# A third expert stage with four buffers, two banks for spread and sum, and second products five blocks behind

## The chip, the cores and the metric

The kernel runs on one core of a Trainium2 chip. The core has a matrix engine (PE), a vector engine (DVE), a scalar engine (ACT), a general engine (POOL) and a queue that issues transfers (SP). Each engine takes its instructions in the order in which they were written; between engines only semaphores hold work back. Products are written to eight banks of PSUM, each of 128 x 512 float32 numbers here. The metric is the time of one execution on the device, in microseconds (us).

## The reference

Four layers of a small model work on 2048 tokens of width 128; each layer is a mixing step and then a feed-forward step, both on a normalised input and both added back. The change touches the feed-forward step of the third layer only, a mixture of 8 experts with 256 hidden units, of which each token uses two:

```python
logits = xf @ Wg + bg
probs = jax.nn.softmax(logits, axis=-1)
w, idx = jax.lax.top_k(probs, TOP_K)
w = w / jnp.sum(w, axis=-1, keepdims=True)
comb = jnp.sum(jax.nn.one_hot(idx, E, dtype=xf.dtype) * w[..., None], axis=1)
h = jax.nn.relu(jnp.einsum('nd,edh->enh', xf, W1) + b1[:, None, :])
y = jnp.einsum('enh,ehd->end', h, W2) + b2[:, None, :]
out = jnp.einsum('end,ne->nd', y, comb)
```

The kernel computes all experts for all tokens and weighs the hidden units by `comb`, which is zero for experts that a token does not use.

## The kernel before

The tokens are cut into four chunks of 512 (`NC` = 4, `CH` = 512). The stage of the third layer is called FFN2; its 8 x 256 hidden units are 16 blocks of 128, two for each expert. For each chunk `c` and block `b` (number `n` over all of them) the work is this, with features along the partitions and tokens along the 512 columns:

- **first product** (`up`, PE): the block's 128 x 128 weights by the normalised input, into the gate bank `n % 2`. Every product is three matmuls (`mm3`, lines 731 to 733), since weights and inputs are each held as a high and a low part: high by high, high by low, low by high.
- **activation** (`act`, ACT, line 913): bias and Relu from the gate bank into `AO[n % 2]`.
- **spread** (`spread`, PE, line 866): for every second block one matmul that copies an expert's routing weights to all 128 partitions, into the one bank `SP`. It waits until the weighing before it has read the bank.
- **weighing** (`weigh`, DVE, line 968): the activation times the spread bank, into `HO[n % 3]`. It waits until the low part of block n-3 has been made.
- **high part** (`high`, ACT, line 921): a rounded copy of the weighed block into `rbuf[n % 2]`. It waits until the second product of block n-2 has been read from there.
- **low part** (`low`, POOL, line 989; the last two of the stage on DVE): weighed block minus high part, into `rbuf[2 + n % 2]`.
- **second product** (`down`, PE, lines 731 to 733 again): three matmuls that add the block's share to the sum in the one bank `Y`. The first block of a chunk is led by two matmuls with the second bias (lines 877 and 878), and waits until ACT has copied the chunk before out of `Y` (`result`, line 926).

The order within an engine is written out. On PE iteration `b` issues `up(b)`, for even b `spread(b)`, and then `down(b - 3)`, because `_f.lag` is 3. On ACT it issues `act(b)` and `high(b - 1)`, on DVE `weigh(b)`, on POOL `low(b - 2)`. After that come the steps of other work that `hooks` puts at this block, by the table `STEPS_AT`: for the chunk after this one the routing weights, for the chunk two further the normalisation. Steps 0, 1, 11, 2 and 3 are that normalisation (statistics on DVE, a small power on POOL at lines 497 and 498, the scaling on DVE at line 406, four transposes on PE at line 698, the split into high and low on ACT and DVE). Step 4 is twelve narrow matmuls for the logits (lines 719 to 721), 5 to 9 the choice of the two experts (ACT and DVE, lines 444 to 481; the last of them, at b = 11, makes `SC2` in four small copies and four small subtractions, lines 478 and 481), and 10 the four transposes of `SC2` on PE (line 726) with ACT's copy of them into `SCT` (line 545), from which the next chunk's spreads read. The step -1 is the tail of the chunk before: four transposes of its sum on PE (line 749) at b = 3, and the addition on DVE (line 762) at b = 4. POOL also splits the weights of later stages into high and low after every third block, as long as there are any (`work`, lines 2117 and 2118). During the last chunk `hook(EARLY + b)` adds the first five products of the next stage ("keys"), with ACT's copies at line 1606 and DVE's splits at lines 1619 and 1621.

The first chunk starts while the stage before ends; the stage after starts when ACT has copied the last chunk's sum (line 926). For the other two expert stages, which have two first products for each block, the same functions are used with `f.gate` set.

Of the kernel before, what the change touches and what calls it, by code (L numbers as in the profile page):

```python
# [132 lines left out]
for _f in FFNS:  # L133
    _f.block0, _f.spread0, _f.router0 = _blk, _sp, _rt
    _blk += NC * _f.blocks
    _sp += NC * _f.spread
    _rt += NC * (1 if _f.experts else 0)
    _f.lag = 3
ROUTED = {f.norm: f for f in FFNS if f.experts}


def build(nc, x_in, w_split, w_exact, w_raw, out):
    with ExitStack() as ctx:
# [635 lines left out]
        AO = [buf[0], buf[1]]  # L779
        MO = [buf[2], buf[3]]  # L780
        HO = [buf[4], buf[5], buf[6]]

        def body_start(eng, t, c):

# [13 lines left out]
        def in_stage(f, c, b, depth):  # L798
# [5 lines left out]

# [3 lines left out]
        }  # L808
        EARLY = 20
        ALL_STEPS = (0, 1, 11, 2, 3, 4, 5, 6, 7, 8, 9, 10)  # L810
# [19 lines left out]
        def ffn_pe(pe, f, c, hook):  # L830
# [24 lines left out]
            def spread(c, b):  # L855
                if b == f.plain_block or b % f.spread_every:
                    return
                n = block_no(f, c, b)
                if b == 0:
                    pe.wait_ge(weights_sb, f.router0 + c + 1)  # L860
                if in_stage(f, c, b, 1):
                    pe.wait_ge(h_ready, n)
                elif f is FFN2:
                    body_start(pe, f.tail, 0)
                o = EXACT_AT["sel16"][0] + b // f.spread_every * P
                nc.tensor.matmul(SP[:, :], WE[:, o:o + P], SCT[:, bass.ds(c % 2 * CH, CH)],  # L866
                                 start=True, stop=True).then_inc(spread_full, 1)

            def down(c, b):
                n = block_no(f, c, b)  # L870
                if b == 0:
                    y_bank_free(pe, f.tail, c)
                    if f.experts == 8:

                        s = SCT[:, bass.ds(c % 2 * CH, CH)]
                        bh, bl = wh("b2_2")
                        nc.tensor.matmul(Y[:, :], bh, s, start=True, stop=False)
                        nc.tensor.matmul(Y[:, :], bl, s, start=False, stop=False)
# [18 lines left out]
        def ffn_act(a, chain, f, c, hook):  # L897
# [6 lines left out]
            def act(c, b):  # L904
                n = block_no(f, c, b)
                a.wait_ge(first_full, n + 1)
                if in_stage(f, c, b, 2):

                    a.wait_ge(mul_done if f.gate else h_ready, n - 1)
                if f.gate:  # L910
                    nc.scalar.activation(AO[n % 2], G[n % 2][:, :], ACT.Silu).then_inc(act_done, 1)  # L911
                else:
                    nc.scalar.activation(AO[n % 2], G[n % 2][:, :], ACT.Relu, bias=raw("b1_2", b, 1))\  # L913
                        .then_inc(act_done, 1)

            def high(c, b):
                n = block_no(f, c, b)
                a.wait_ge(h_ready, n + 1)
                if in_stage(f, c, b, 2):
                    a.wait_ge(down_done, n - 1)  # L920
                nc.scalar.activation(rbuf[n % 2][:, :], HO[n % 3], ACT.Copy).then_inc(hh_ready, 1)  # L921

            def result(c):
                yt_free(a, f.tail, c)
                a.wait_ge(down_done, block_no(f, c, f.blocks - 1) + 1)
                nc.scalar.activation(YT[:, :], Y[:, :], ACT.Identity, bias=zero).then_inc(yt_ready, 1)
# [17 lines left out]
        def ffn_dve(v, chain, f, c, hook):  # L944
# [12 lines left out]
            def weigh(c, b):  # L957

                n = block_no(f, c, b)
                v.wait_ge(mul_done if f.gate else act_done, n + 1)  # L960
                if in_stage(f, c, b, 3):
                    v.wait_ge(hl_ready, n - 2)
                src = MO[n % 2] if f.gate else AO[n % 2]
                if b == f.plain_block:
                    nc.vector.tensor_copy(HO[n % 3], src).then_inc(h_ready, 1)
                else:
                    v.wait_ge(spread_full, f.spread0 + f.spread * c + b // f.spread_every + 1)
                    nc.vector.tensor_tensor(HO[n % 3], src, SP[:, :], ALU.mult).then_inc(h_ready, 1)  # L968

            for b in range(f.blocks):  # L970
                if f is FFN0 and (c, b) == (0, 1):
# [12 lines left out]
        def low(e_, eng, f, n):  # L984

            eng.wait_ge(hh_ready, n + 1)
            if e_ is nc.vector and n:
                eng.wait_ge(hl_ready, n)
            e_.tensor_tensor(rbuf[2 + n % 2][:, :], HO[n % 3],  # L989
                             rbuf[n % 2][:, :].bitcast(F32), ALU.subtract).then_inc(hl_ready, 1)  # L990

        def low_on_pool(f, c, b):

# [1311 lines left out]
```

## Time and profile before

| what | value |
|---|---|
| three executions, median | 897.65 us |
| lowest and highest of them | 897.23 and 898.66 us |
| the profiled execution | 897.48 us |
| its span, first to last instruction | 895.7 us |
| busy PE, DVE, ACT, POOL over the span | 734.7, 675.6, 575.3, 394.1 us |
| mean granted TensorE clock | 0.911 |

The profiled execution took 897.48 us, of which the span of instructions is 895.7 us; the rest lies before and after them. The stage of the change fills some 145 us of it, from the first weighing at 452.7 us to the copy of the last sum at 598.0 us. A matmul of 512 columns is listed with 0.39 to 0.40 us although the next one starts 0.23 us after it, since matmuls are pipelined: what PE costs is read from start to start.

### The profile page before, as it was taken

What the parts mean: (1) busy time and instruction counts of PE and PEld (TensorE: products, weight loads), DVE (VectorE), ACT (ScalarE), POOL (GpSimd) and SP (SyncE); (2) the same over time, 40 slices, a digit from 0 to 9 for tenths busy, and PEclk for the clock granted to TensorE, in tenths of its full rate; (3) what the DMA queues carried; (4) which work ended last, traced back from release to release, by engine and by line L of the source; (5) the groups of instructions that cost most, each with busy time, mean ns of one, the idle gap of its engine ahead of it and who ended that gap; (6) DMA issues with size and microseconds to landing.
All of it is one profiled execution on the core that took longest, in us unless ns stands there. A gap on an engine that the chain in (4) does not pass through costs nothing. (4 is left out here: it accounts for less than half of the span.)

```text
span 895.7 us, 11019 instructions
## 1 busy us (share of the span) xinstructions
PE 734.7 (82%) x3306; PEld 467.0 (52%) x3306; DVE 675.6 (75%) x1615; ACT 575.3 (64%) x926; POOL 394.1 (44%) x427
## 2 busy tenths in 40 slices
PE   4778998779999889999678888867777767777787
PEld 3666765345545567777555666642232222222575
DVE  6685776798898748787756667769898788786785
ACT  4264664657474535565636667767899979777776
POOL 6638654634445015544248767634333332230330
PEclk9999998988696869999969999998999889789999
DMA  4200001000000000000000000000000000000001
GB/s 134 69 12 15 15 15 33 19 23 24 12 25 19 1 0 1 1 1 0 1 13 23 1 1 0 1 0 1 1 0 1 1 1 0 1 0 1 1 1 48
DMA packets 9610, 11.59 MB, mean 13 GB/s; under 512 B 720, under 2 KB 5712, under 8 KB 9552
## 3 DMA queue, kind: packets, MB, share of 16 engines
q1 hardware_dynamic: 9552, 10.89, 4.2%
q8 instruction: 27, 0.44, 0.2%
q14 instruction: 31, 0.25, 0.1%
HBM read 9.84 MB, written 1.05 MB: 12 GB/s over the span
## 5 line engine op out<-in xcount | busy, mean ns | idle before, releaser
L989 POOL TENSOR_TENSOR rbuf<-B,rbuf 128x512 fp32r<-128x512 f32 x126 | 164.2, 1307 | 101.8 <-ACT rbuf L921 101.0
L968 DVE TENSOR_TENSOR B<-B,spread_bank 128x512 f32<-128x512 f32 x128 | 87.1, 682 | 47.2 <-ACT B L913 33.0
L921 ACT ACTIVATE rbuf<-B 128x512 fp32r<-128x512 f32 x132 | 83.0, 628 | 49.0 <-PE y_bank L733 38.8
L497 POOL TENSOR_SCALAR small<-small 128x4 f32<-128x4 f32 x32 | 8.1, 252 | 175.9 <-DVE small L387 175.7
L731 PE MATMUL y_bank<-rbuf,WH 128*128 128x512 f32 x150 | 64.2, 428 | 20.8 <-POOL rbuf L989 14.4
L955 DVE TENSOR_TENSOR B<-B,up_banks 128x512 f32<-128x512 f32 x68 | 46.5, 684 | 45.4 <-PE up_banks L733 28.5
L911 ACT ACTIVATE B<-gate_banks 128x512 f32<-128x512 f32 x68 | 40.8, 599 | 61.6 <-PE gate_banks L733 60.4
L1715 ACT ACTIVATE B<-B,VEC 128x1024 f32<-128x1024 f32 x48 | 55.2, 1150 | 22.3 <-DVE B L1710 22.3
L731 PE MATMUL gate_banks<-XH,WH 128*128 128x512 f32 x152 | 66.7, 439 | 0.8 <-ACT YT L1313 0.8
L733 PE MATMUL gate_banks<-XH,WL 128*128 128x512 f32 x152 | 62.4, 411 | 0.0
L732 PE MATMUL gate_banks<-XL,WH 128*128 128x512 f32 x152 | 61.9, 407 | 0.0
L1203 POOL TENSOR_SCALAR B<-S,WR 128x128 f32<-128x128 f32 x64 | 39.2, 629 | 49.7 <-DVE S L1185 38.1
L733 PE MATMUL y_bank<-rbuf,WL 128*128 128x512 f32 x150 | 60.2, 402 | 0.0
L732 PE MATMUL y_bank<-rbuf,WH 128*128 128x512 f32 x150 | 60.0, 400 | 0.0
L1617 POOL TENSOR_SCALAR WH<-WK 128x512 fp32r<-128x512 f32 x22 | 13.8, 628 | 104.6 <-issue 57.9
L1244 PEld LDWEIGHTS spread_bank<-VB,B 128*128 128x128 f32 x256 | 37.6, 226 | 34.1 <-issue 26.2
L866 PE MATMUL spread_bank<-SCT,WE 128*128 128x512 f32 x96 | 42.6, 444 | 10.7 <-DVE B L968 8.7
L1716 ACT ACTIVATE B<-B 128x1024 f32<-128x1024 f32 x48 | 50.5, 1052 | 0.0
L913 ACT ACTIVATE B<-gate_banks,WR 128x512 f32<-128x512 f32 x64 | 43.8, 687 | 10.0 <-PE gate_banks L733 9.5
L731 PEld LDWEIGHTS y_bank<-rbuf,WH 128*128 128x128 f32 x150 | 28.9, 193 | 40.2 <-POOL rbuf L989 23.2
L1221 PE MATMUL gate_banks<-B,S 128*64 128x512 f32 x128 | 44.6, 786 | 5.3 <-issue 3.8
L1244 PE MATMUL spread_bank<-VB,B 128*128 128x36 f32 x256 | 41.1, 314 | 2.0 <-DVE Z L1380 2.0
(318 smaller groups left out, 2110.8 us busy)
## 6 DMA issues: line engine op xcount, KB each, us to landing
STG<-in_w_split SPq DMA_DIRECT2D x27, 256.0 KB, 2.7
X<-in_x SPq DMA_DIRECT2D x4, 256.0 KB, 4.6
out<-X SPq DMA_DIRECT2D x4, 256.0 KB, 2.3
WR<-in_w_raw SPq DMA_DIRECT2D x1, 524.5 KB, 4.0
STG<-in_w_exact SPq DMA_DIRECT2D x2, 256.0 KB, 2.7
STG<-in_w_split SPq DMA_DIRECT2D x5, 64.0 KB, 1.9
STG<-in_w_split SPq DMA_DIRECT2D x1, 192.0 KB, 2.3
STG<-in_w_split SPq DMA_DIRECT2D x1, 128.0 KB, 2.1
```

The lines of the kernel that those rows point to most:

```text
L731: nc.tensor.matmul(dst, w[0], x[0], start=start, stop=False)
L732: nc.tensor.matmul(dst, w[0], x[1], start=False, stop=False)
L733: return nc.tensor.matmul(dst, w[1], x[0], start=False, stop=stop)
L913: nc.scalar.activation(AO[n % 2], G[n % 2][:, :], ACT.Relu, bias=raw("b1_2", b, 1))\
L921: nc.scalar.activation(rbuf[n % 2][:, :], HO[n % 3], ACT.Copy).then_inc(hh_ready, 1)
L955: nc.vector.tensor_tensor(MO[n % 2], AO[n % 2], U[n % 2][:, :], ALU.mult).then_inc(mul_done, 1)
L968: nc.vector.tensor_tensor(HO[n % 3], src, SP[:, :], ALU.mult).then_inc(h_ready, 1)
L989: e_.tensor_tensor(rbuf[2 + n % 2][:, :], HO[n % 3], rbuf[n % 2][:, :].bitcast(F32), ALU.subtract).then_inc(hl_ready, 1)
L1221: i = nc.tensor.matmul(G[u][w * WIN:(w + 1) * WIN, :], QN[c_ % 2][:, tok], KM[tile % 2][:, HU * u:HU * u + HU, w * WIN:(w + 1) * WIN], sta ...
L1244: i = nc.tensor.matmul(SP[:, pr * 36:(pr + 1) * 36], PT[u][:, q * P:(q + 1) * P], VB[:, tile % TL, pr, :, :, :].rearrange("p a b d -> p (a ...
L1715: nc.scalar.activation(CS[p % 4], AB[p % 4], ACT.Sin, scale=-TURN, bias=half_pi).then_inc(cos_ready, 1)
L1716: nc.scalar.activation(SN[p % 4], RB[p % 4], ACT.Sin, scale=-TURN).then_inc(sin_ready, 1)
```

## The change

The second products of FFN2 stand five blocks behind the first ones, not three (`_f.lag`). Activations, weighed blocks, high and low parts of this stage have four buffers each: `AO4` and `HO4` take eight of the slots of `B`; two of the four high and low parts are `rbuf` as before, and two lie in columns of `WH` and `WL` whose weights (the taps and those of the second layer) are no longer read. The spread has the bank `SP` and the second half of `up_banks`, in turn; the sum has `Y` for even chunks and the first half of `up_banks` for odd ones, so that only chunks 2 and 3 wait for a copy, that of the chunk two before. The high part is made two blocks behind the activation instead of one. The waits follow: `act(n)` waits for the weighing n-4 (before: n-2), `weigh(n)` for the low part n-4 (n-3), `high(n)` for the second product n-4 (n-2), a spread for the weighing three blocks back (one). Step 10 is at b = 14 instead of 13. By the lag, the copy of a chunk's sum moves from b = 2 of the next chunk to b = 4 on ACT, its transposes from b = 3 to b = 5 on PE, and its addition from b = 4 to b = 6 on DVE. Number and size of the instructions stay as they are.

```diff
-    _f.lag = 3
+    _f.lag = 5 if _f is FFN2 else 3
...
+        MADE_H, MADE_L = (w_[:, _end - 2 * CH:_end] for w_ in (WH, WL))
+        AO4, HO4 = [buf[k] for k in range(4)], [buf[4 + k] for k in range(4)]
+        HI4 = [rbuf[0][:, :], rbuf[1][:, :], MADE_H[:, 0:CH], MADE_H[:, CH:2 * CH]]
+        LO4 = [rbuf[2][:, :], rbuf[3][:, :], MADE_L[:, 0:CH], MADE_L[:, CH:2 * CH]]
+        SP2, Y2 = [SP[:, :], U[1]], [Y[:, :], U[0]]
...
+            return AO4[n % 4] if deep_of(f) else AO[n % 2]
...
+            return HO4[n % 4] if deep_of(f) else HO[n % 3]
...
+            return (HI4[n % 4], LO4[n % 4]) if deep_of(f) else (rbuf[n % 2][:, :], rbuf[2 + n % 2][:, :])
...
+            return SP2[b // f.spread_every % 2] if deep_of(f) else SP[:, :]
...
+            return Y2[c % 2] if deep_of(f) else Y[:, :]
...
-            16: {0: (0,), 1: (4,), 2: (1,), 3: (5,), 4: (11,), 5: (6,), 7: (2, 7), 8: (3,), 9: (8,), 11: (9,), 13: (10,)},
+            16: {0: (0,), 1: (4,), 2: (1,), 3: (5,), 4: (11,), 5: (6,), 7: (2, 7), 8: (3,), 9: (8,), 11: (9,), 14: (10,)},
...
-                if in_stage(f, c, b, 1):
+                if deep_of(f) and in_stage(f, c, b, 4):
+                    pe.wait_ge(h_ready, n - 2)
+                elif deep_of(f):
+                    body_start(pe, f.tail, 0)
+                elif in_stage(f, c, b, 1):
                     pe.wait_ge(h_ready, n)
-                elif f is FFN2:
-                    body_start(pe, f.tail, 0)
...
                 if b == 0:
-                    y_bank_free(pe, f.tail, c)
+                    if not deep_of(f):
+                        y_bank_free(pe, f.tail, c)
+                    elif c > 1:
+                        pe.wait_ge(yt_ready, count(f.tail, c - 1))
...
-                mm3(Y[:, :], wh(f.down, b * P), (rbuf[n % 2][:, :], rbuf[2 + n % 2][:, :]),
+                mm3(dst, wh(f.down, b * P), parts(f, n),
                     b == 0 and f.experts != 8, b == f.blocks - 1).then_inc(down_done, 1)
...
+                    if in_stage(f, c, b, 4):
+                        a.wait_ge(h_ready, n - 3)
+                    nc.scalar.activation(act_out(f, n), G[n % 2][:, :], ACT.Relu, bias=raw("b1_2", b, 1))\
                         .then_inc(act_done, 1)
...
                 a.wait_ge(h_ready, n + 1)
-                if in_stage(f, c, b, 2):
+                if deep_of(f):
+                    if in_stage(f, c, b, 4):
+                        a.wait_ge(down_done, n - 3)
+                elif in_stage(f, c, b, 2):
                     a.wait_ge(down_done, n - 1)
...
-                for at_ in lagged(f, c, b, 2 if f.gate else 1):
+                for at_ in lagged(f, c, b, 2):
                     high(*at_)
...
-                if in_stage(f, c, b, 3):
+                if deep_of(f):
+                    if in_stage(f, c, b, 4):
+                        v.wait_ge(hl_ready, n - 3)
+                elif in_stage(f, c, b, 3):
                     v.wait_ge(hl_ready, n - 2)
```

The order on PE around the first second product of chunk 1. In the kernel before, after `up(3)`; `y_bank` is the sum's bank, and each row names in brackets what it waits for:

```order
L731 MATMUL gate_banks<-XH,WH 128x512 [waits act_done]
L732 MATMUL gate_banks<-XL,WH 128x512
L733 MATMUL gate_banks<-XH,WL 128x512
L877 MATMUL y_bank<-SCT,WH 128x512 [waits yt_ready]
L878 MATMUL y_bank<-SCT,WL 128x512
L731 MATMUL y_bank<-rbuf0,WH 128x512 [waits hl_ready]
L732 MATMUL y_bank<-rbuf2,WH 128x512
L733 MATMUL y_bank<-rbuf0,WL 128x512
L749 MATMUL norm_bank<-WR,YT 128x128 [waits res_done,x32_ready,yt_ready]
L749 MATMUL norm_bank<-WR,YT 128x128 x3
```

In the changed kernel, after `up(5)`:

```order
L731 MATMUL gate_banks<-XH,WH 128x512 [waits act_done]
L732 MATMUL gate_banks<-XL,WH 128x512
L733 MATMUL gate_banks<-XH,WL 128x512
L912 MATMUL up_banks<-SCT,WH 128x512
L913 MATMUL up_banks<-SCT,WL 128x512
L731 MATMUL up_banks<-rbuf0,WH 128x512 [waits hl_ready]
L732 MATMUL up_banks<-rbuf2,WH 128x512
L733 MATMUL up_banks<-rbuf0,WL 128x512
L749 MATMUL norm_bank<-WR,YT 128x128 [waits res_done,x32_ready,yt_ready]
L749 MATMUL norm_bank<-WR,YT 128x128 x3
```

The two bias matmuls and the product now go to the other bank, without a wait for the copy of chunk 0 (`yt_ready`), and the transposes of that copy still follow directly behind the product, two blocks later than before.

PE around the transposes of the routing weights, the step that moved by one block. Before, `down(10)`, the step, and `up(14)` with its spread:

```order
L731 MATMUL y_bank<-rbuf0,WH 128x512 [waits hl_ready]
L732 MATMUL y_bank<-rbuf2,WH 128x512
L733 MATMUL y_bank<-rbuf0,WL 128x512
L726 MATMUL route_bank<-WR,SC2 128x128 [waits weights_tok]
L726 MATMUL route_bank<-WR,SC2 128x128 x3
L731 MATMUL gate_banks<-XH,WH 128x512 [waits act_done]
L732 MATMUL gate_banks<-XL,WH 128x512
L733 MATMUL gate_banks<-XH,WL 128x512
L866 MATMUL spread_bank<-SCT,WE 128x512 [waits h_ready]
```

In the changed kernel, `up(14)` with its spread, `down(9)`, and the step:

```order
L731 MATMUL gate_banks<-XH,WH 128x512 [waits act_done]
L732 MATMUL gate_banks<-XL,WH 128x512
L733 MATMUL gate_banks<-XH,WL 128x512
L897 MATMUL up_banks<-SCT,WE 128x512 [waits h_ready]
L731 MATMUL y_bank<-rbuf1,WH 128x512 [waits hl_ready]
L732 MATMUL y_bank<-rbuf3,WH 128x512
L733 MATMUL y_bank<-rbuf1,WL 128x512
L726 MATMUL route_bank<-WR,SC2 128x128 [waits weights_tok]
L726 MATMUL route_bank<-WR,SC2 128x128 x3
```

`up(14)` and its spread stood behind the step and stand ahead of it now; what lies between the step and the next chunk is `up(15)` and `down(10)` (`up(14)`, `down(11)`, `up(15)` and `down(12)` before).

## Rows read from the trace of the kernel before

**Rows 1.** Busy time by stretch, from each chunk's first weighing to the next one's:

```profile
core 0: us, PE busy (x) PEld busy (x) DVE busy (x) ACT busy (x) POOL busy (x), PEclk, DMA share, GB/s
452.68:490.33 37.65, 32.07 (x123) 23.30 (x121) 23.67 (x61) 21.01 (x34) 28.18 (x27) 0.86 0.08 22
490.33:525.20 34.87, 30.05 (x132) 21.99 (x133) 23.36 (x59) 22.41 (x36) 26.28 (x23) 1.00 0.00 1
525.20:559.20 34.00, 29.51 (x132) 21.80 (x131) 23.39 (x72) 22.53 (x36) 23.39 (x21) 1.00 0.00 0
559.20:593.80 34.60, 30.57 (x129) 22.21 (x127) 24.04 (x51) 24.65 (x39) 22.40 (x20) 1.00 0.00 1
```

**Rows 2.** Waits from 484 to 596 us: total, times, longest, in us:

```profile
ACT rbuf L921 <- PE y_bank L733: 27.4, 30, 2.2
DVE B L968 <- ACT B L913: 25.4, 24, 2.1
POOL rbuf L989 <- ACT rbuf L921: 23.7, 27, 1.6
...
PE route_bank L726 <- DVE SC L481: 2.2, 3, 0.8
...
PE y_bank L877 <- ACT YT L926: 1.3, 2, 0.7
```

**Rows 3.** PE in order of time: start, duration, line, operands:

```profile
484.50 0.66 PE L726 MATMUL route_bank<-WR,SC 128*128 128x128 f32 x4 [0.58 <-DVE SC L481]
484.91 0.47 PE L731 MATMUL gate_banks<-XH,WH 128*128 128x512 f32 x1
...
492.54 0.17 PE L719 MATMUL route_bank<-WH,XH 128*128 128x8 f32 x1
...
493.79 0.48 PE L731 MATMUL gate_banks<-XH,WH 128*128 128x512 f32 x1
...
497.25 0.50 PE L877 MATMUL y_bank<-SCT,WH 128*128 128x512 f32 x1 [0.67 <-ACT YT L926]
...
497.82 0.40 PE L731 MATMUL y_bank<-rbuf,WH 128*128 128x512 f32 x1
...
578.28 0.39 PE L866 MATMUL spread_bank<-SCT,WE 128*128 128x512 f32 x1
578.51 0.40 PE L731 MATMUL y_bank<-rbuf,WH 128*128 128x512 f32 x1
...
579.22 0.39 PE L731 MATMUL route_bank<-XH,WH 128*128 128x512 f32 x1
```

**Rows 4.** ACT in order of time, at the end of the stage:

```profile
592.38 0.63 ACT L921 ACTIVATE rbuf<-B 128x512 fp32r<-128x512 f32 x1 [0.66 <-PE y_bank L733]
593.01 0.69 ACT L913 ACTIVATE B<-gate_banks,WR 128x512 f32<-128x512 f32 x1
593.77 0.63 ACT L921 ACTIVATE rbuf<-B 128x512 fp32r<-128x512 f32 x1
...
597.96 0.69 ACT L926 ACTIVATE YT<-y_bank,VEC 128x512 f32<-128x512 f32 x1 [1.84 <-PE y_bank L733]
```

**Rows 5.** POOL in order of time, at the start and within the first chunk:

```profile
456.50 0.19 POOL L497 TENSOR_SCALAR small<-small 128x4 f32<-128x4 f32 x1 [13.99 <-DVE small L387]
...
457.76 1.27 POOL L989 TENSOR_TENSOR rbuf<-B,rbuf 128x512 fp32r<-128x512 f32 x1
...
479.66 0.62 POOL L2117 TENSOR_SCALAR WH<-STG 128x512 fp32r<-128x512 f32 x1
...
481.64 2.51 POOL L989 TENSOR_TENSOR rbuf<-B,rbuf 128x512 fp32r<-128x512 f32 x2
```

**Rows 6.** DVE in order of time: start, duration, line, operands:

```profile
449.02 0.41 DVE L478 CAST SC<-small 128x16 fp32r<-128x16 f32 x4
...
480.35 2.59 DVE L478 CAST SC<-small 128x16 fp32r<-128x16 f32 x4
482.97 1.47 DVE L481 TENSOR_TENSOR SC<-small,SC 128x16 f32<-128x16 f32 x4
...
496.10 3.56 DVE L406 TENSOR_SCALAR XN<-X,small 128x128 f32<-128x128 f32 x4
```

More of the change, by code:

```diff
@@ L781, in build, with deep_of, act_out, hidden @@
         HO = [buf[4], buf[5], buf[6]]
+        MADE_H, MADE_L = (w_[:, _end - 2 * CH:_end] for w_ in (WH, WL))
[3 more added lines that the diff above has]
+        SP2, Y2 = [SP[:, :], U[1]], [Y[:, :], U[0]]
+        def deep_of(f):
+            return f is FFN2
+        def act_out(f, n):
+            return AO4[n % 4] if deep_of(f) else AO[n % 2]
+        def hidden(f, n):
+            return HO4[n % 4] if deep_of(f) else HO[n % 3]
+        def parts(f, n):
+            return (HI4[n % 4], LO4[n % 4]) if deep_of(f) else (rbuf[n % 2][:, :], rbuf[2 + n % 2][:, :])
+        def spread_bank(f, c, b):
+            return SP2[b // f.spread_every % 2] if deep_of(f) else SP[:, :]
+        def sum_bank(f, c):
+            return Y2[c % 2] if deep_of(f) else Y[:, :]
         def body_start(eng, t, c):
@@ L870, in down @@
                 n = block_no(f, c, b)
+                dst = sum_bank(f, c)
                 if b == 0:
-                    y_bank_free(pe, f.tail, c)
+                    if not deep_of(f):
+                        y_bank_free(pe, f.tail, c)
+                    elif c > 1:
+                        pe.wait_ge(yt_ready, count(f.tail, c - 1))
                     if f.experts == 8:
@@ L876, in down @@
                         bh, bl = wh("b2_2")
-                        nc.tensor.matmul(Y[:, :], bh, s, start=True, stop=False)
-                        nc.tensor.matmul(Y[:, :], bl, s, start=False, stop=False)
+                        nc.tensor.matmul(dst, bh, s, start=True, stop=False)
+                        nc.tensor.matmul(dst, bl, s, start=False, stop=False)
                 pe.wait_ge(hl_ready, n + 1)
-                mm3(Y[:, :], wh(f.down, b * P), (rbuf[n % 2][:, :], rbuf[2 + n % 2][:, :]),
+                mm3(dst, wh(f.down, b * P), parts(f, n),
                     b == 0 and f.experts != 8, b == f.blocks - 1).then_inc(down_done, 1)
@@ L906, in act @@
                 a.wait_ge(first_full, n + 1)
-                if in_stage(f, c, b, 2):
-                    a.wait_ge(mul_done if f.gate else h_ready, n - 1)
                 if f.gate:
-                    nc.scalar.activation(AO[n % 2], G[n % 2][:, :], ACT.Silu).then_inc(act_done, 1)
-                else:
-                    nc.scalar.activation(AO[n % 2], G[n % 2][:, :], ACT.Relu, bias=raw("b1_2", b, 1))\
+                    if in_stage(f, c, b, 2):
+                        a.wait_ge(mul_done, n - 1)
+                    nc.scalar.activation(act_out(f, n), G[n % 2][:, :], ACT.Silu).then_inc(act_done, 1)
+                else:
+                    if in_stage(f, c, b, 4):
+                        a.wait_ge(h_ready, n - 3)
+                    nc.scalar.activation(act_out(f, n), G[n % 2][:, :], ACT.Relu, bias=raw("b1_2", b, 1))\
                         .then_inc(act_done, 1)
@@ L918, in high @@
                 a.wait_ge(h_ready, n + 1)
-                if in_stage(f, c, b, 2):
+                if deep_of(f):
+                    if in_stage(f, c, b, 4):
+                        a.wait_ge(down_done, n - 3)
+                elif in_stage(f, c, b, 2):
                     a.wait_ge(down_done, n - 1)
-                nc.scalar.activation(rbuf[n % 2][:, :], HO[n % 3], ACT.Copy).then_inc(hh_ready, 1)
+                nc.scalar.activation(parts(f, n)[0], hidden(f, n), ACT.Copy).then_inc(hh_ready, 1)
             def result(c):
@@ L925, in result @@
                 a.wait_ge(down_done, block_no(f, c, f.blocks - 1) + 1)
-                nc.scalar.activation(YT[:, :], Y[:, :], ACT.Identity, bias=zero).then_inc(yt_ready, 1)
+                nc.scalar.activation(YT[:, :], sum_bank(f, c), ACT.Identity, bias=zero).then_inc(yt_ready, 1)
             for b in range(f.blocks):
@@ L988, in low @@
                 eng.wait_ge(hl_ready, n)
-            e_.tensor_tensor(rbuf[2 + n % 2][:, :], HO[n % 3],
-                             rbuf[n % 2][:, :].bitcast(F32), ALU.subtract).then_inc(hl_ready, 1)
+            hi, lo = parts(f, n)
+            e_.tensor_tensor(lo, hidden(f, n), hi.bitcast(F32), ALU.subtract).then_inc(hl_ready, 1)
         def low_on_pool(f, c, b):
```

8 lines of the change are left out of this document (4 added, 4 removed).

## The prediction

> **What bounds the kernel now.** I read first the busy time by stretch, cut at each chunk's first weighing [rows 1]. A chunk of the stage takes 37.7, 34.9, 34.0 and 34.6 us, the last one counted only to its last weighing, and in none of them is an engine full: in the second, PE is busy for 30.1 us, POOL for 26.3, DVE for 23.4 and ACT for 22.4. The granted clock is 1.00 from the second chunk on, 2.4 GHz, so the idle time does not cost clock there. PE's 30.1 us count the ends of pipelined matmuls; what it needs comes from starts.
>
> Then the waits [rows 2]: ACT's high part waits 30 times, 27.4 us, for a second product on PE; DVE's weighing 24 times, 25.4 us, for the activation on ACT; POOL's low part 27 times, 23.7 us, for the high part on ACT. Each engine waits for the next one round a ring. That is what a loop with too few buffers looks like: second product n-2, high part n, low part n, second product n. The ring is short of places, not of engine time.
>
> **What each engine needs for a chunk.** PE, from start to start [rows 3]: a product of three matmuls is 579.22 - 578.51 = 0.71 us; I use 0.70, as the time between two starts there is 0.23 to 0.24. A spread is 578.51 - 578.28 = 0.23, the two bias matmuls 497.82 - 497.25 = 0.57, the twelve logit matmuls 493.79 - 492.54 = 1.25, four transposes 484.91 - 484.50 = 0.41. A middle chunk has 32 products, 8 spreads, the bias, the logits and three groups of transposes: 22.4 + 1.8 + 0.6 + 1.25 + 1.2 = 27.3 us. The last chunk has no logits and no routing weights to transpose, but five products and four transposes for the next stage: 22.4 + 1.8 + 0.6 + 1.2 + 3.5 = 29.5 us.
>
> ACT has a high part and an activation in 593.77 - 592.38 = 1.39 us [rows 4], 0.07 more than their 0.63 and 0.69 us; 16 times that on top of its busy 22.4 us makes 23.5 us. POOL has a low part in half of 2.51 us, 1.26 us, so 20.1 us for 16. A split piece of a later weight takes 481.64 - 479.66 = 1.98 us and the small pair of the normalisation 457.76 - 456.50 = 1.26 us [rows 5]. The first chunk has five such pieces, one of them half as large (9.4 us, as I estimate it), the second two. DVE's busy time is the 23.4 to 24.0 us of rows 1. So with enough buffers PE is the bound in the second to fourth chunk, and POOL in the first.
>
> **The change, part by part.** No instruction is added or dropped; it only moves waits.
>
> Four buffers and lag 5. The activation, weighing, high part and low part of a block take 0.69 + 0.69 + 0.63 + 1.26 = 3.3 us [rows 4, 5] (the weighing is 0.69 too, as ACT's activation; it is the same size). In the new order the high part of block n stands on ACT behind the activation of block n+2, two blocks of PE or some 3.0 us later; so from the end of `up(n)` to the end of its low part I count 3.0 + 0.7 + 0.1 + 0.63 + 1.26 = 5.7 us, with 0.1 for the semaphore. `down(n)` comes five blocks of 1.51 us behind, 7.6 us. Nearly 2 us of slack are left in a full PE, and about 4 us for a late weighing, since the high part waits for its turn anyway. With lag 3 PE arrived after 4.5 us, and every hold of DVE reached it at once. Four buffers for the activation let ACT and PE run on by two blocks more while DVE is held. I take these waits as gone except where DVE is held longer than that.
>
> The second sum bank. The waits of PE for ACT's copy are 1.3 us in this stretch [rows 2], once for each chunk change; they go. The second spread bank takes the spread's wait for the weighing just before it. Both are parts of PE's idle 34.9 - 27.3 = 7.6 us and are not counted again.
>
> What stays late: DVE. Its operations from SBUF to SBUF stretch while POOL works. The four small copies of step 9 took 0.41 us with POOL idle at 449 us, but 2.59 us at 480 us, and the four subtractions behind them 1.47 us; the four scalings at 496 us took 3.56 us [rows 6]. POOL gets denser, so I count them as held in every chunk. Step 9 then holds DVE for 4.1 us and 0.7 us of small operations ahead of them, 4.8 us, behind `weigh(11)`. At the end of `weigh(11)` PE is in block 12, with about 4 us of work until `down(9)`, which is just ahead of the transposes. DVE comes to the step late by another 0.4 us or so, from splitting the input at b = 8. So PE waits 1.2 us there, although the step is one block later; it was 2.2 us in three [rows 2], so this wait grows by 0.5. Behind it, `up(15)` and `down(10)` cover the copy into `SCT` less well than the four products of before; weighing 12, high part 12 and the copy, which I take at a high part's length, take 0.69 + 0.63 + 0.63 = 1.95 us against 0.4 + 3 x 0.7 = 2.5 us of PE, so it stays hidden.
>
> The tail. The transposes at b = 5 fill the norm bank, DVE empties it at b = 6, and step 2 needs it on PE at b = 7. Before there were three blocks between them. From the end of `up(6)` PE needs 0.23 + 3 x 0.7 = 2.3 us to step 2, DVE's chain activation, weighing, addition 0.2 + 0.69 + 0.69 + 0.69 = 2.3 us, and DVE is still late from the scalings at b = 2. I take 1.0 us of waiting; it is between 0 and the 3.6 us of the scalings.
>
> Together PE needs 27.3 + 1.2 + 1.0 = 29.5 us for a middle chunk. The second falls from 34.9 to 29.5, a gain of 5.4 us, the third from 34.0, 4.5 us.
>
> The first chunk. The half clock at its start (0.86 as mean of the stretch, 1.2 GHz in part) and the late first low part at 457.76 are as before. From there POOL needs 20.1 + 9.4 = 29.5 us and perhaps 1 us of holds, so the next chunk's first low part can start at 488.3; its weighing stands some 3 us earlier, at 485.3 instead of 490.3. Gain 5.0 us.
>
> The last chunk. From first to last weighing PE has 15 of 16 blocks, 29.5 - 1.5 = 28.0 us, and 1.0 us for the tail step: 29.0 instead of 34.6, 5.6 us. Behind the last activation, though, come six second products and three high parts, two of them one block later than before; POOL's low part 13 ends later and DVE's two wait for it. From the last activation to the copy there were 597.96 - 593.01 = 4.95 us [rows 4]; I add 0.6 us.
>
> Sum: 5.0 + 5.4 + 4.5 + 5.6 - 0.6 = 19.9 us. The stages behind start that much earlier and are not touched. The profiled execution took 897.48 us, 0.17 below the median of 897.65, which changes nothing: 897.5 - 19.9 = **877.6 us**; I say 878.
>
> **A rule that speaks against it.** The held DVE operations are on the trace as said [rows 6]. The Trainium skill ("SBUF — State Buffer", section "Who interferes with whom") says why: VectorE and GpSimd share one pair of SBUF ports under a lock that is held for a whole instruction, and the loser stands still; it concerns copies and scalings in the fast modes and operations with two inputs in SBUF. The trace agrees in that four copies went from 0.41 to 2.59 us. Read strictly it would make every such operation wait out one POOL instruction once POOL has no gaps, and that is the rival "slower" below. The weighing has one input in PSUM and stays out of it by the same rule.
>
> **The rivals.**
>
> *DVE becomes the bound.* It is busy for 23.4 us while POOL is busy for three quarters of the stretch [rows 1]. With POOL at nine tenths more of the small operations are held: half of another 4.1 + 3.6 us gives 27 us, and DVE keeps at least 5 us of waits at the ends of its holds, where PE and ACT have run dry. A chunk is then 32.5 us: gains of 2, 2.4, 1.5 and 3, less 0.6, some 8.5 us, **889 us**. For it: held operations come in pairs, at b = 8 and 11. Against it: POOL pauses in chunks three and four, where it needs only 21.4 us of 29.5.
>
> *PE runs full.* The two waits that I put in do not show. Middle chunks at 27.3 us, the last at 28.0 and the first with 2 us less: 7 + 7.6 + 6.7 + 6.6 - 0.6 = 27 us, **870 us**. Against it: the transposes of the routing weights wait already now.
>
> *Slower: each held operation waits out a whole low part.* Step 9 has nine such operations; nine times 1.26 us is 11.3 us instead of 4.8 us. The scalings take 4 x 1.26 = 5.0 instead of 3.6 us, and the input's split and one more subtraction some 1.5 us more. DVE has 23.4 + 6.5 + 1.4 + 1.5 = 33 us for a chunk, 2 us of it idle besides: 35 us, and 38 us in the third chunk, which scales twice. Against 34.9 and 34.0 us that is 4 us longer in all, **901 us**. The point from which it decides: four held copies end with the fourth POOL instruction. Those of rows 6 ended at 482.94, 2.59 us or two low parts of 1.26 us after their start, and POOL would pause as soon as DVE is late, which is why I give it little.
>
> *Nothing changes.* Another wait of the same size closes the ring, for instance the high parts on ACT for the second products four back. Then the stage keeps its 34 us, **897 us**. The places above leave no such ring in a full PE.
>
> **How the numbers follow.** Forecast 0.60, DVE as the bound 0.20, full PE 0.10, slower 0.05, nothing 0.05. The bounds of the unknown costs are 0 to 3.6 us for each tail step and 0 to 2.5 us for each step 9. The range from 869 to 889 us holds the forecast and reaches both neighbours. A difference of 0.2%, 1.8 us, is about what the runs can tell from none. Faster than that: 0.60 + 0.20 + 0.10 = 0.90; the same 0.05; slower 0.05.
>
> **What would show it.** Right: chunks of 29 to 30 us between first weighings from the second on, PE's starts at 0.23 us in runs of many products, waits of ACT for second products nearly gone, waits of PE for step 9 (line 726) at about 1 us a chunk, and of step 2 for the addition. The forecast is wrong if DVE shows no waits and copies of 5 us or more in step 9, if POOL waits as often for ACT as now, or if the granted clock in the stage falls below 1.00 behind its first chunk.

## The result and the profile after

| | before | changed |
|---|---|---|
| executions, median | 898.15 us | 886.71 us |
| lowest and highest | 897.23 and 898.83 us | 885.71 and 889.12 us |
| the profiled execution, and its span | 897.48, 895.7 us | 885.71, 883.9 us |
| stage, first weighing to the last copy | 145.3 us | 134.1 us |
| mean granted clock | 0.911 | 0.903 |

The kernel before has one execution more here than in the table ahead of the prediction. The ratio is 0.9884, with a 95% interval of 0.9857 to 0.9911: the change makes the kernel 11.4 us faster. Of the 11.8 us of span, 11.2 lie in the stage; the first weighing came 0.8 us earlier, at 451.90 us, and the work behind the last copy took 297.9 us, as against 297.7. Between runs the first weighing starts anywhere from 448.7 to 459.8 us, with nothing changed ahead of it, so below I compare kernels by the stage's length as well as by their time. The stage's length is that of one execution, the profiled one.

Busy time by stretch in the changed kernel, again from first weighing to first weighing, the last stretch to the last weighing (they answer to [rows 1]):

```profile
core 0: us, PE busy (x) PEld busy (x) DVE busy (x) ACT busy (x) POOL busy (x), PEclk, DMA share, GB/s
451.90:486.33 34.43, 30.87 (x118) 24.01 (x117) 25.80 (x62) 19.59 (x34) 26.90 (x26) 0.80 0.09 24
486.33:515.80 29.47, 28.24 (x133) 22.77 (x132) 24.16 (x59) 21.15 (x37) 26.53 (x24) 0.99 0.01 1
515.80:547.95 32.15, 27.99 (x131) 22.24 (x130) 28.19 (x72) 21.30 (x37) 23.29 (x21) 1.00 0.00 1
547.95:581.46 33.51, 29.76 (x128) 24.01 (x127) 27.89 (x51) 23.44 (x39) 22.28 (x20) 0.95 0.00 1
```

The second chunk takes 29.5 us, which is the forecast. The third and fourth take 32.2 and 33.5 us, not 29.5 and 29.0, and DVE is busy in them for 28 us instead of 23.4 and 24.0. DVE does the same work there: it is held more. Its waits from 484 to 586 us, and those of the others (they answer to [rows 2]):

```profile
ACT B L949 <- PE gate_banks L733: 16.7, 34, 1.5
DVE B L1010 <- ACT B L949: 15.8, 18, 2.1
POOL rbuf L1032 <- ACT rbuf L960: 9.2, 11, 2.0
POOL WL L1032 <- ACT WH L960: 8.9, 6, 4.0
...
PE norm_bank L698 <- DVE X L762: 7.1, 2, 3.7
```

ACT's 27.4 us of waits for second products are gone, it waits for first products instead. The new row is the last one: PE waits twice, for 7.1 us, at the transposes of the normalisation (line 698, step 2) for the addition of the tail on DVE (line 762). On PE in order of time, the two waits, the wait at the routing weights in the first chunk, and what follows two of them:

```profile
479.59 0.40 PE L733 MATMUL y_bank<-rbuf,WL 128*128 128x512 f32 x1
481.81 0.66 PE L726 MATMUL route_bank<-WR,SC 128*128 128x128 f32 x4 [1.82 <-DVE SC L481]
...
484.09 0.63 PE L731 MATMUL gate_banks<-XH,WH 128*128 128x512 f32 x1
484.51 0.63 PE L732 MATMUL gate_banks<-XL,WH 128*128 128x512 f32 x1
...
512.26 0.66 PE L726 MATMUL route_bank<-WR,SC 128*128 128x128 f32 x4 [1.23 <-DVE SC L481]
...
532.59 0.63 PE L698 MATMUL norm_bank<-WR,XN 128*128 128x128 f32 x4 [3.34 <-DVE X L762]
...
565.37 1.09 PE L698 MATMUL norm_bank<-WR,XN 128*128 128x128 f32 x4 [3.75 <-DVE X L762]
566.11 0.78 PE L731 MATMUL gate_banks<-XH,WH 128*128 128x512 f32 x1
566.68 0.63 PE L732 MATMUL gate_banks<-XL,WH 128*128 128x512 f32 x1
```

Behind the wait of 1.82 us the matmuls start 0.42 us apart instead of 0.23, from 483.24 to 486.65 us: the granted clock has fallen to half, 1.2 GHz. The same follows the wait of 3.75 us, from 565.16 to 568.57 us, but not the ones of 1.23 and 3.34 us. Each fall costs some 1.7 us, half of the 3.4 us that it lasts. In the kernel before, PE was idle for 4.8 us of the second chunk in many small pieces and kept its full clock [rows 1]; in the changed kernel, where few waits are left, two of the longer ones lost it. What DVE did ahead of the wait in the third chunk:

```profile
525.24 0.69 DVE L1010 TENSOR_TENSOR B<-B,spread_bank 128x512 f32<-128x512 f32 x1
525.84 4.81 DVE L416 TENSOR_SCALAR XN<-Z,small 128x128 f32<-128x128 f32 x4
530.57 0.67 DVE L1010 TENSOR_TENSOR B<-B,spread_bank 128x512 f32<-128x512 f32 x1
531.17 0.67 DVE L1010 TENSOR_TENSOR B<-B,up_banks 128x512 f32<-128x512 f32 x1
531.77 0.67 DVE L762 TENSOR_TENSOR X<-X,norm_bank 128x512 f32<-128x512 f32 x1
```

and POOL in the same time:

```profile
525.56 1.29 POOL L1032 TENSOR_TENSOR rbuf<-B,rbuf 128x512 fp32r<-128x512 f32 x1
526.80 2.55 POOL L1032 TENSOR_TENSOR WL<-B,WH 128x512 fp32r<-128x512 f32 x2
529.30 1.27 POOL L1032 TENSOR_TENSOR rbuf<-B,rbuf 128x512 fp32r<-128x512 f32 x1
```

Taken one by one in the trace, the four scalings ended at 526.93, 528.18, 529.43 and 530.65 us, and the four low parts at 526.85, 528.10, 529.35 and 530.57: each scaling waited out one low part and ended 0.08 us behind it. So semaphores are not all that holds an engine back here, as the section on the chip has it. In the kernel before, the same four took 1.41 us:

```profile
536.50 1.41 DVE L416 TENSOR_SCALAR XN<-Z,small 128x128 f32<-128x128 f32 x4
...
534.53 2.52 POOL L989 TENSOR_TENSOR rbuf<-B,rbuf 128x512 fp32r<-128x512 f32 x2
537.62 2.68 POOL L989 TENSOR_TENSOR rbuf<-B,rbuf 128x512 fp32r<-128x512 f32 x2 [0.57 <-ACT rbuf L921]
```

Only the first of them met a low part, the one that ended at 537.05; then POOL stood still for 0.57 us behind ACT, and the other three took 0.34 us each. The four scalings are step 11, at b = 4, which only the last two chunks have, and the weighings 5 and 6 and the addition come behind them. The addition ended at 532.44, and PE, which had been ready since 529.25, went on at 532.59.

### The profile page after: what moved, and what is told of

The parts are those of the page before. It is cut to its first block and busy times, and to the rows that moved or that the text cites. A ratio compares the mean times of both kernels' runs of the same rounds, so it can differ in the third digit from the quotient of the medians.

```text
span 883.9 us, 11015 instructions
## 1 busy us (share of the span) xinstructions
PE 731.3 (83%) x3306; PEld 469.4 (53%) x3306; DVE 686.8 (78%) x1615; ACT 570.6 (65%) x926; POOL 394.5 (45%) x427
## 5 line engine op out<-in xcount | busy, mean ns | idle before, releaser
L1032 POOL TENSOR_TENSOR rbuf<-B,rbuf 128x512 fp32r<-128x512 f32 x96 | 124.1, 1295 | 83.6 <-ACT rbuf L960 83.4
L960 ACT ACTIVATE rbuf<-B 128x512 fp32r<-128x512 f32 x100 | 62.5, 625 | 17.3 <-DVE B L1010 12.3
L1010 DVE TENSOR_TENSOR B<-B,spread_bank 128x512 f32<-128x512 f32 x96 | 64.7, 678 | 11.0 <-ACT B L949 7.0
L949 ACT ACTIVATE B<-gate_banks,WR 128x512 f32<-128x512 f32 x64 | 44.0, 689 | 27.3 <-PE gate_banks L733 26.7
L731 PE MATMUL y_bank<-rbuf,WH 128*128 128x512 f32 x102 | 43.8, 430 | 11.6 <-POOL rbuf L1032 5.9
L1032 POOL TENSOR_TENSOR WL<-B,WH 128x512 fp32r<-128x512 f32 x30 | 39.9, 1342 | 9.0 <-ACT WH L960 8.9
L2160 POOL TENSOR_TENSOR WL<-STG,WH 128x512 fp32r<-128x512 f32 (+3 forms) x34 | 40.5, 1192 | 2.8
L733 PE MATMUL y_bank<-rbuf,WL 128*128 128x512 f32 x102 | 41.1, 403 | 0.0
L1371 ACT ACTIVATE B<-B 128x512 f32<-128x512 f32 x32 | 20.1, 629 | 32.4 <-DVE B L1440 32.0
```

The source lines that it names most:

```text
L731: nc.tensor.matmul(dst, w[0], x[0], start=start, stop=False)
L733: return nc.tensor.matmul(dst, w[1], x[0], start=False, stop=stop)
L949: nc.scalar.activation(act_out(f, n), G[n % 2][:, :], ACT.Relu, bias=raw("b1_2", b, 1))\
L960: nc.scalar.activation(parts(f, n)[0], hidden(f, n), ACT.Copy).then_inc(hh_ready, 1)
L1010: nc.vector.tensor_tensor(hidden(f, n), src, spread_bank(f, c, b), ALU.mult).then_inc(h_ready, 1)
L1032: e_.tensor_tensor(lo, hidden(f, n), hi.bitcast(F32), ALU.subtract).then_inc(hl_ready, 1)
```

## The experiments

All start from the changed kernel unless said. "Stage" is the length from the first weighing to the last copy in the profiled execution: 145.3 us before, 134.1 us changed.

### Which wait costs: steps moved, holds taken away

**e1**, steps 2 and 3 later:

```diff
-            16: {0: (0,), 1: (4,), 2: (1,), 3: (5,), 4: (11,), 5: (6,), 7: (2, 7), 8: (3,), 9: (8,), 11: (9,), 14: (10,)},
+            16: {0: (0,), 1: (4,), 2: (1,), 3: (5,), 4: (11,), 5: (6,), 7: (7,), 9: (8, 2), 10: (3,), 11: (9,), 14: (10,)},
```

> The changed kernel with one edit: the normalisation's transposes (step 2) stand at b = 9 instead of 7, and the split behind them (step 3) at b = 10 instead of 8. Theory A (PE waits at step 2 for the addition on DVE, which stands behind a held scaling, in chunks 2 and 3): the 7.1 us of waits at line 698 go, and the half clock behind the second of them too (1.5 us); chunks 2 and 3 fall from 32.2 and 33.5 to 29.5 and 30 us; time 887 - 6 = 881 us (879 to 883). Theory B (DVE is simply full in these chunks): the waits reappear at line 726 or at the second products, and the time stays at 885 to 888 us.

Median 881.96 us, ratio 0.9812 (0.9761 to 0.9862); stage 128.8 us. The waits at line 698 are gone, the fourth chunk took what theory A said and the third 1.2 us more, both with the clock at 1.00:

```profile
512.51:543.22 30.71, 28.16 (x131) 22.27 (x130) 27.22 (x71) 21.13 (x37) 23.26 (x21) 1.00 0.00 1
543.22:572.94 29.72, 28.68 (x128) 22.71 (x127) 27.90 (x51) 23.15 (x39) 22.42 (x20) 1.00 0.00 1
```

DVE is as busy as ever (27.2 and 27.9 us), so it is not the bound; what cost was that PE needed the addition at that place. In its stead PE waits 2.3 us for weighings, 1.35 of them behind the second scaling of the third chunk. The intervals of e1 and of the changed kernel overlap a little, and the profiled execution was the fastest of six (876.41 us). What settles it are the waits, and that e3 and e11, which move step 2 too (and change step 9), lie wholly below the changed kernel.

**e2**, POOL's low parts cut to 8 of 512 columns:

```diff
-            e_.tensor_tensor(lo, hidden(f, n), hi.bitcast(F32), ALU.subtract).then_inc(hl_ready, 1)
+            k_ = 8 if f is FFN2 and e_ is nc.gpsimd else CH
+            e_.tensor_tensor(lo[:, 0:k_], hidden(f, n)[:, 0:k_], hi[:, 0:k_].bitcast(F32), ALU.subtract).then_inc(hl_ready, 1)
```

> The changed kernel, but POOL makes only 8 of the 512 columns of each low part in this stage, so its output is not the reference's. POOL is then nearly idle there and can hold nothing. Both theories: the copies and subtractions of step 9 take 0.4 us each again and the scalings 1.1 to 1.4 us. Theory A and B alike say that PE then has no waits of note in the middle chunks: 27.5 to 28 us each, the first some 31, the last 29, time about 877 us (874 to 880). If the time hardly falls (884 or more), the holds by POOL are not what costs, and the prediction's account of DVE is wrong.

869.61 us, ratio 0.9675 (0.9633 to 0.9717); stage 116.6 us, more than expected:

```profile
451.46:481.39 29.93, 29.14 (x119) 23.55 (x118) 20.90 (x62) 19.48 (x34) 13.04 (x26) 0.82 0.10 27
481.39:508.79 27.40, 27.40 (x131) 22.41 (x130) 18.51 (x59) 21.08 (x37) 8.32 (x22) 1.00 0.01 1
508.79:536.20 27.41, 27.41 (x131) 22.42 (x130) 19.43 (x71) 21.16 (x37) 5.68 (x20) 1.00 0.00 1
536.20:564.39 28.19, 28.19 (x128) 22.89 (x127) 20.25 (x51) 23.18 (x39) 5.47 (x19) 1.00 0.00 1
```

The time is below the expected 874 to 880 us. PE is busy for all of 27.40 us and has no wait of note in the stage; its need had been worked out as 27.3. DVE falls from 28.2 to 19.4 us in the third chunk, so 9 us of its busy time there were holds, and its second scaling takes 1.11 us instead of 4.81:

```profile
517.85 1.11 DVE L416 TENSOR_SCALAR XN<-Z,small 128x128 f32<-128x128 f32 x4
```

In the first two chunks POOL still splits weights, and DVE's small work is still held there: the four copies of step 9 take 1.53 us in the first, the four scalings 2.52 and 2.40 us. This kernel also makes the low parts themselves short, so it gives the price of POOL's low parts in all, 17.5 us of stage, not of the holds alone.

**e3**, every step away from PE's need of it:

```diff
+            16: {0: (0,), 1: (4,), 2: (1,), 3: (5,), 4: (11,), 5: (6,), 7: (7, 8), 8: (2,), 9: (9,), 11: (3,), 14: (10,)},
```

> The changed kernel with the steps spread so that no held one stands just ahead of PE's need of it: step 8 with 7 at b = 7, step 2 at b = 8, step 9 at b = 9, step 3 at b = 11, step 10 at b = 14 as it is. Theory A: DVE has five blocks between step 9 and step 10, so the 3.6 us of waits at line 726 go, and most of those at line 698; chunks of 28 to 29.5 us, time 878 us (876 to 881). Theory B: 885 to 888 us, with PE waiting for low parts instead.

879.88 us, ratio 0.9788 (0.9747 to 0.9828); stage 128.4 us, chunks of 32.5, 30.8, 30.0 and 30.6 us. The time is theory A's, the chunks are longer than its 28 to 29.5 us. No wait at line 726 was left, and 1.3 us at line 698. But theory B had something too: PE waited eight times for low parts, 4.2 us in all and up to 1.32 us, and the second chunk is longer than in the changed kernel.

**e4**, step 10 one block earlier, as it was before (`13: (10,)`):

> The changed kernel with step 10 back at b = 13. PE comes to the transposes one block (1.5 us) earlier while DVE ends step 9 at the same time: Theory A: each of the three waits at line 726 grows by 1 to 1.5 us, 3 to 4.5 us in all, and the clock may fall more often; 890 us (888 to 893). Theory B: PE has slack for it, 886 to 888 us.

897.74 us, ratio 0.9986 (0.9961 to 1.001); stage 142.3 us. In time the whole gain is gone: 11 us where I had expected 3. Of the stage's gain 3 us are left. The three waits at line 726 are 3.42, 2.87 and 2.06 us instead of 1.82, 1.23 and 0.53, 4.8 us more. The clock did the rest of the 8.1 us: behind the stretch at half clock that the first chunk starts with, it fell to half four times and not twice, for 3.4 us each, and two falls more cost 3.4 us. Behind the first wait:

```profile
489.63 0.90 PE L726 MATMUL route_bank<-WR,SC 128*128 128x128 f32 x4 [3.42 <-DVE SC L481]
490.18 0.78 PE L731 MATMUL gate_banks<-XH,WH 128*128 128x512 f32 x1
490.75 0.63 PE L732 MATMUL gate_banks<-XL,WH 128*128 128x512 f32 x1
491.18 0.63 PE L733 MATMUL gate_banks<-XH,WL 128*128 128x512 f32 x1
```

Its third chunk ran at a mean clock of 0.91 and took 36.8 us.

**e9**, that edit alone in the kernel before (`14: (10,)` instead of 13):

> The kernel before with one edit: step 10 at b = 14 instead of 13. If the later step is by itself what the change brought (it was worth 8 us of stage with lag 5 and four buffers: 142.3 against 134.1), the stage falls from 145.3 to 137 to 139 us and the time to 890 us. If it only counts once PE runs ahead of DVE, as I expect, no more than PE's 2.2 us of waits at line 726 can go: stage 143 to 145 us, 897 us, not told from before.

899.05 us, ratio 1.0006 (0.9982 to 1.0029); stage 146.1 us. PE's 2.2 us of waits at line 726 are gone, but its waits for weighings rose from 5.3 to 8.9 us. The later step is worth 8 us of stage with the rest of the change and nothing without it.

### Which part is needed: each undone alone

**e5**, the distance as before:

```diff
-    _f.lag = 5 if _f is FFN2 else 3
+    _f.lag = 3
...
-                for at_ in lagged(f, c, b, 2):
+                for at_ in lagged(f, c, b, 2 if f.gate else 1):
                     high(*at_)
```

> The changed kernel with the second products three blocks behind and the high parts one block behind, as before; four buffers, two banks each and step 10 at b = 14 stay. Theory A (distance covers the holds of DVE, more than places do): the chain activation, weighing, high, low leaves 0.3 us of slack in a full PE, so each hold of 3.5 to 4.8 us reaches PE; stage 139 to 142 us (134.1 in the changed kernel, 145.3 before), time 892 us (889 to 896). Theory C (the buffers bring it, the lag little): stage 133 to 136 us, 886 us.

885.93 us, ratio 0.9871 (0.9848 to 0.9894), the same as the changed kernel; stage 136.1 us. Theory C held for the time: the lag brings some 2 us of stage in these two profiles, and nothing that the times can tell. PE pays elsewhere: it waits 13.5 us for low parts, 8 times for `y_bank` alone, and not at all at line 726 nor for the addition, whose place is then b = 4 (rows from 455 to 588 us):

```profile
PE y_bank L731 <- POOL rbuf L1032: 5.5, 6, 1.8
...
PE y_bank L731 <- POOL WL L1032: 3.4, 2, 2.0
```

So lag 5 took nearly all of these waits away (1.8 us are left) and brought 7.1 us of others by moving the tail, and 3.6 us at line 726, where PE now comes ahead of DVE.

**e6**, one bank for the sum (`sum_bank` gives `Y`, and `y_bank_free` is called as before):

> The changed kernel with one bank for the sum, and PE's wait for the copy of the chunk before. The copy takes 0.7 us and PE has one product of 0.7 us between, so each of three waits is 0.3 to 0.8 us: 1.5 us at most, 887 to 889 us against 887; not told from none. If it is over 3 us slower, the wait met a late ACT, or set off the clock.

889.84 us, ratio 0.9914 (0.9884 to 0.9944); stage 136.3 us, of which the third chunk has 34.7 at a clock of 0.90. The interval reaches over that of the changed kernel, so the times leave open whether the second sum bank brings 0 or 6 us. The profile says that it spares little: PE waits for the copy twice, 0.5 us in all. The waits at lines 726 and 698 are those of the changed kernel (3.6 and 7.1 us), and the clock is at half for one stretch of 3.4 us more.

**e7**, one bank for the spread, each waiting for the weighing before it:

> The changed kernel with one bank for the spread, which waits for the weighing just before it as in the kernel before. Theory A: PE is tied to DVE at every second block, so lag and buffers can't cover a hold: each hold of 2 to 4.8 us reaches PE; chunks of 33 to 35 us, stage 141 to 145 us, time 896 us (892 to 902). If 888 or less, the second spread bank is not needed with lag 5.

900.33 us, ratio 1.0027 (1.0007 to 1.0048): theory A, and a little slower than the kernel before. Stage 146.9 us, 2 us more than expected; the half clock of the first chunk lasts 6.8 us longer than in the changed kernel. PE waits for the weighing 15 times:

```profile
PE spread_bank L897 <- DVE B L1010: 19.9, 15, 2.4
```

**e8**, two high and two low parts, `high` waiting for the second product n-2:

> The changed kernel with two high and two low parts as before, lag 5 and the rest kept. The high part of block n then waits for the second product n-2, which PE issues behind the first product n+3: 0.4 us of slack are left of 1.9. Theory A: the waits of ACT for second products come back, and a hold reaches PE about 1.5 us sooner; stage 137 to 140 us, 890 us (888 to 894). If 887 or less, the four high and low parts bring nothing beside the lag.

899.17 us, ratio 1.0007 (0.9987 to 1.0028), stage 142.7 us: a loss of 8.6 us of stage where 3 to 6 were expected, and in time all of the gain. The ring of [rows 2] is back; over the whole stage ACT waits 45 us for second products, 34 in the kernel before (the rows are of 455 to 588 us):

```profile
ACT rbuf L957 <- PE y_bank L733: 22.4, 25, 2.5
ACT rbuf L957 <- PE up_banks L733: 19.4, 19, 2.9
```

What four places for activations and weighed blocks bring was not tried alone: no run has two of the one or three of the other with the rest of the change.

### Mending it

**e10**, the four copies and four subtractions of step 9 as one instruction each:

```diff
-            parts = [slice(0, TL)] if D_ == 1 else [slice(k, k + 1) for k in range(TL)]
+            parts = [slice(0, TL)]
...
-            (lambda t5, k, h_: t5[:, k.start, h_, :, :])
+            (lambda t5, k, h_: t5[:, :, h_, :, :])
...
-            (lambda k: rwd[:, k.start, :, :])
+            (lambda k: rwd)
```

> The changed kernel with the four copies and four subtractions of step 9 for this stage written as one instruction each (same elements). A hold costs by the instruction, so step 9 falls from 4.3 to 5 us to about 2.5 us, and the 3.6 us of waits at line 726 go, with the half clock behind the first of them (3.4 us at half speed, 1.7 us): stage 129 to 131 us, 882 us. If holds cost by the element or by POOL's share, step 9 stays over 4 us and nothing changes.

886.3 us, ratio 0.9856 (0.9825 to 0.9888); stage 133.9 us. The hold did go by the instruction: in the first chunk copy and subtraction took 1.8 us instead of 4.45:

```profile
474.16 1.22 DVE L478 CAST SC<-small 128x64 fp32r<-128x64 f32 x1
475.42 0.57 DVE L481 TENSOR_TENSOR SC<-small,SC 128x64 f32<-128x64 f32 x1
```

and two of three waits at line 726 went. The first chunk fell from 34.4 to 32.3 us. The rest of the expectation failed: the second rose by 0.8 us, with small waits for low parts. The third and fourth took 33.0 and 33.7 us, since the waits for the addition (3.33 and 3.75 us) stand unchanged in them, and the first of those now lost the clock too. Alone it is not told from the changed kernel.

**e11**, e1 and e10 together:

> Both mends together: steps 2 and 3 at b = 9 and 10, step 9 in one copy and one subtraction. The sums of e1 (5.3 us) and of e10 (3 to 5 us): stage 124 to 126 us, against 118 for the kernel with POOL's low parts cut to 8 columns; 877 us. It should beat both kernels.

880.26 us, ratio 0.979 (0.9755 to 0.9825); stage 127.1 us. Its interval lies wholly below that of the changed kernel: it beats both. The expectation was 1 to 3 us too good.

```profile
452.54:484.85 32.31, 30.26 (x120) 23.48 (x119) 22.99 (x56) 19.90 (x34) 25.05 (x24) 0.82 0.09 25
484.85:515.19 30.34, 28.33 (x131) 22.08 (x130) 22.81 (x53) 21.23 (x37) 28.19 (x25) 1.00 0.00 1
515.19:545.41 30.22, 28.18 (x131) 22.27 (x130) 26.73 (x66) 21.14 (x37) 23.26 (x21) 1.00 0.00 1
545.41:575.12 29.71, 28.72 (x128) 22.73 (x127) 27.91 (x51) 23.14 (x39) 22.43 (x20) 1.00 0.00 1
```

What is left above 27.4 us is small waits of PE for low parts and for weighings behind the second scaling, none over 1.4 us, and POOL's load in the first two chunks.

**e12**, the same with `_f.lag = 4`:

> As the one before, with the second products four blocks behind. The tail then comes one block earlier and a block of slack less is left for low parts. With lag 3 and no mends PE waited 9 us for low parts in this stage; I expect 2 to 4 us of such waits, stage 125 to 129 us, 877 to 880 us: no better than lag 5 with the mends. If the lag covers nothing beyond four, it is equal.

884.33 us, ratio 0.9835 (0.9804 to 0.9866); stage 130.8 us: worse than expected. PE waits 7.7 us for low parts in the stage, 3.4 in e11. Of the 3.7 us over e11, 4.0 are in the first chunk (36.3 us), where POOL also splits weights; PE waits there up to 1.53 us for a low part, and behind that wait the clock is at half for 3.4 us, which it is not in e11. The two intervals overlap; the executions themselves overlap by 1 us only (876.6 to 881.8 us in e11, 880.8 to 886.5 us here). With the other waits mended, the fifth block of distance counts.

## Why the prediction was right, and where it was off

The time lay in the range, though near its upper end, and the direction was right. So was the mechanism, a ring short of places; but the gain was 11.4 us and not 19.9. Of the stage's gain, 5.0, 5.4, 4.5 and 5.6 us were forecast for the four chunks and 0.6 us of loss for the end; measured from weighing to weighing they are 3.3, 5.4, 1.8, 1.0 and 0.3 us, 8.7 us less in all. By its own steps:

- **PE's need, 27.3 us for a middle chunk**: right; 27.4 us when POOL is out of the way (e2).
- **The ring goes**: right. ACT's waits for second products are gone, and they come back when the parts are two again (e8). The sum took all the places together and so did not show how they depend on each other: taking the four parts or the second spread bank away costs 8.6 and 12.8 us of the stage's 11.2, and in time all the gain each (e8, e7).
- **The second chunk, 29.5 us**: right, and in part by luck. The wait at line 726 was 1.2 us as forecast (1.23). The wait for the tail was 0 there, not 1.0; what made up for it seems to be the end of the half clock, which lasts until 486.65 us. From one pass of PE at line 726 to the next, 481.81 to 512.26, are 30.45 us: 1.23 of waiting, some 1.7 of half clock, and 27.5.
- **The tail, 1.0 us of waiting, "between 0 and the 3.6 us of the scalings"**: this is the term that failed. It was 3.34 and 3.75 us in the third and fourth chunk, the last beyond the upper bound. I took the scalings at b = 2, which I had seen held in the second chunk; in the last two the second scaling of step 11 stands at b = 4, two weighings ahead of the addition. It had cost 1.41 us in the trace, and in the sum I did not ask what it would cost with POOL busy; the rival "slower" did, and names the third chunk, which scales twice. Against the 3 us of the sum the waits are 7.1 us, and with the half clock behind the second of them (1.7 us) that makes 5.8 of the 8.7 us. With step 2 later the chunks fell to 30.7 and 29.7 us and the stage by 5.3 us (e1).
- **The rival "slower", each held operation waits out a low part**: its mechanism was right for the scalings (4.81 us for four), and half right for step 9 (1.93 + 2.52 us for eight): of the eight in the first chunk four ended 0.03 us behind an instruction of POOL, and the other four took 0.16 us each. Its price was not, since PE ran ahead far enough for all holds but those just ahead of its need. The rule of the Trainium skill that I set beside it ("SBUF — State Buffer", "Who interferes with whom": one lock for the whole instruction, the loser stands still) agrees with the trace here, down to the single instruction: one copy of the same elements took 1.2 us, where four had taken up to 2.6 (e10). The weighing, which the rule leaves out, took 0.65 to 0.69 us throughout.
- **The first chunk, 5.0 us**: 3.25. The wait at line 726 was 1.82 us and took the clock with it; POOL was not the only bound. In e10, without both, the chunk fell by another 2.1 us, to 32.3, about what was forecast (32.6). The sum also took the first low part as starting "as before"; in the changed kernel it starts 8.1 us after the first weighing and not 5.1, since its high part stands behind the activation two blocks later.
- **The clock**: not in the sum at all. A clock below 1.00 behind the first chunk was one of my signs of a wrong forecast, and it showed: 0.99 in the second chunk, where the first fall ends, and 0.95 in the fourth. It fell to half twice, behind waits of 1.82 and 3.75 us, for 3.4 us each, some 3.4 us lost in all. The sign "29 to 30 us from the second chunk on" held for the second alone.
- **Moving step 10**: I counted one block of delay as a part of the whole and gave it no price. It is worth 8.1 us of stage (e4), since PE, running ahead, meets DVE's hold at this place first; before, it was worth nothing (e9).
- **Lag 5** brings next to nothing as made (e5), since it moves the tail into the hold. With the tail's reader out of the way and step 9 merged, it brings 3.7 us of stage over lag 4, 1.7 of them by the clock (e11 and e12). Lag 3 with these mends was not tried.
- **The end, 0.6 us longer**: 0.33.

The rival "DVE becomes the bound", 889 us, was near in time and wrong in kind: with DVE about as busy as before the two chunks lost another 5.2 us when steps 2 and 3 moved (e1).

## What to carry to other kernels

When a ring of waits is widened, the engine that was slowed by it runs ahead until it meets the next thing that it needs from the slow one; list these places in its order, and price at each what stands ahead of it on the other engine, at the duration that it will have once the idle neighbour is busy. Move such a step by a block or two before adding buffers: here one block of delay was worth 8.1 us of stage, nearly as much as the second pair of high and low parts, but only together with them. And where two engines hold each other up by the instruction, write small work as one instruction.

## What the runs showed of the hardware

- A group of four scalings of 128x128 on DVE took 1.11 us with POOL nearly idle, 1.41 us with one low part running at their start and 4.81 us beside four low parts in a row.
- In a nearly full PE, single waits of 1.53 (e12), 1.82, 1.96 (e1), 3.42 (e4) and 3.75 us were followed by 3.4 us at half clock, which cost 1.7 us more; waits of 1.23, 2.87 (e4) and 3.34 us were not, while the same place, line 698, with 3.33 us was in e10. The length of the one wait does not decide it, and what does stays open. So a long wait costs its length and sometimes 1.7 us more.
- The same kernel's time varied more than I had expected: the changed kernel from 885.7 to 889.1 us, e1 from 876.4 to 888.4 us, with the mean granted clock between 0.917 and 0.895 in step with it. Differences under some 4 us are not told by the times; the stage's length of one profile each and its waits are what I have for them.
